# Attention and mixture-of-experts layer on one core: the product with V in two halves of the queries, maxima two tasks further ahead, and two changes merged with it

## The reference

```python
def reference(x, W_qkv, b_qkv, W_out, b_out, w_gate, w1_e, w3_e, w2_e, w1_s, w3_s, w2_s):
    xn = (x - mean(x)) / sqrt(var(x) + 1e-5)
    # attention: 16 heads of 16 channels, 1024 tokens a batch, fp32
    q, k, v = split(xn @ W_qkv + b_qkv)
    q = q * cos + rotate_half(q) * sin; k = k * cos + rotate_half(k) * sin
    attn = softmax(q @ k.T / sqrt(16))
    out = (attn @ v) @ W_out + b_out
    # experts: 16 routed, 4 chosen out of 2 of 4 groups, 2 shared; F = 128
    scores = sigmoid(xn @ w_gate.T)
    w, idx = grouped_top_k(scores)             # 4 a token, weights normalised
    routed = sum over idx of w * (silu(xn @ w1_e.T) * (xn @ w3_e.T)) @ w2_e.T
    shared = (silu(xn @ w1_s.T) * (xn @ w3_s.T)) @ w2_s.T
    return x + out + routed + shared
```

## Time and profile before

| | us |
|---|---|
| median of three runs | 1397.03 (1396.93 to 1402.91) |
| the profiled execution | 1410.99 |
| its span | 1408.4 |
| TensorE busy | 1261.6 (90%) |
| VectorE busy | 1050.5 (75%) |
| ScalarE busy | 735.1 (52%) |
| POOL busy | 506.2 (36%) |

### The profile page before, as it was taken

One profiled execution on the slowest core, in us unless ns is written; L12 is line 12 of the kernel. 1 busy time (PEld: TensorE's weight loads), 2 busy tenths in 40 slices (PEclk: granted clock), 3 DMA queues, 4 the chain that ended last, 5 costly groups with the idle time before them and its releaser, 6 DMA issues. The chain is left out here.

```text
span 1408.4 us, 27771 instructions
## 1 busy us (share of the span) xinstructions
PE 1261.6 (90%) x6717; PEld 645.4 (46%) x6718; DVE 1050.5 (75%) x1715; ACT 735.1 (52%) x1584; POOL 506.2 (36%) x797
## 2 busy tenths in 40 slices
PE   4988927989999999999999999999599999979998
PEld 1544413323333333333333333333488888756665
DVE  5788858868888888888888888888255555537777
ACT  2443311757777777777777777777233333322221
POOL 4665514456132222223131313132277777640000
PEclk9999965989999999999999999999799999989999
DMA  5344453345233213331333223321455555447773
GB/s 176 115 144 147 161 149 84 140 125 177 59 96 78 72 50 95 83 79 48 88 88 76 58 74 95 77 70 53 135 158 157 160 157 159 144 141 233 243 238 127
DMA packets 126755, 169.25 MB, mean 120 GB/s; under 512 B 50109, under 2 KB 98653, under 8 KB 124702
## 3 DMA queue, kind: packets, MB, share of 16 engines
q1 hardware_dynamic: 111358, 126.79, 31.6%
q0 software_dynamic: 15360, 42.04, 9.2%
HBM read 96.58 MB, written 71.64 MB: 119 GB/s over the span
## 5 line engine op out<-in xcount | busy, mean ns | idle before, releaser
L964 DVE TENSOR_REDUCE mx<-pm 128x1 f32<-128x1024 f32 x532 | 626.9, 1219 | 123.6 <-PE pm L1033 113.7
L939 ACT ACTIVATE pr<-pst 128x512 f32<-128x512 f32 x1024 | 535.6, 603 | 228.0 <-PE pst L1057 217.0
L1057 PE MATMUL pst<-qt,kt 50*128 50x512 f32 x1024 | 399.5, 464 | 6.0 <-issue 4.4
L1033 PE MATMUL pm<-kt,qt 48*128 48x512 f32 x1064 | 362.5, 449 | 27.8 <-DVE mx L964 22.1
L1033 PEld LDWEIGHTS pm<-kt,qt 48*128 48x128 f32 x1064 | 169.1, 192 | 275.9 <-DVE mx L964 228.3
L1067 PE MATMUL po<-pr,vt 128*17 128x512 f32 x2048 | 273.7, 607 | 15.0 <-ACT osb L948 12.1
L1057 PEld LDWEIGHTS pst<-qt,kt 50*128 50x128 f32 x1024 | 173.6, 186 | 89.0 <-ACT pr L939 68.4
L1195 POOL DMA_INDIRECT s_y<-ys_c,slot_c x144 | 140.6, 976 | 79.3 <-issue 66.1
L862 POOL CAST mp<-mx 128x16 fp32r<-128x16 f32 x33 | 6.5, 196 | 447.4 <-DVE mx L964 447.4
L1260 PE MATMUL c_pG<-w13s,xt_c 128*128 x576 | 150.1, 384 | 0.0
L884 POOL DMA_INDIRECT s_xg<-p_rows,p_slot x128 | 125.1, 978 | 56.6 <-issue 30.2
(11 more groups left out here) (197 smaller groups left out, 1276.0 us busy)
## 6 DMA issues: line engine op xcount, KB each, us to landing
xg<-s_xg SPq DMA_DIRECT2D x144, 128.5 KB
yg<-s_y SPq DMA_DIRECT2D x32, 512.0 KB, 4.3
kt<-s_k SPq DMA_DIRECT2D x34, 256.0 KB
qt<-s_q SPq DMA_DIRECT2D x68, 128.0 KB
s_q<-stg SPq DMA_DIRECT2D x32, 256.0 KB
s_k<-stg SPq DMA_DIRECT2D x32, 256.0 KB
vt<-s_v SPq DMA_DIRECT2D x17, 272.0 KB, 11.5
w13s<-w SPq DMA_DIRECT2D x1, 4608.0 KB
```

Of the source, the lines that this page charges most:

```text
L939: nc.scalar.activation(pr[:, (k % 2) * 4 + ORDER[i], :], pst[bank(gg, k, i)][:, :], ACT.Exp, scale=SCALE).then_inc(exp_ok, 1)
L964: nc.vector.tensor_reduce(mx[:, half, col:col + 1], pm[slot][:, :, :].rearrange("p a n -> p (a n)"), AX.X, ALU.max).then_inc(mx_free, 1)
L1033: mm = pe.matmul(pm[slot][:, kk, :], qt[buf][rows, half, pair, qi * P:(qi + 1) * P], kt[buf][rows, pair, kk * 512:(kk + 1) * 512], start=T ...
L1057: pe.matmul(pst[bank(buf, k, i)][:, :], kt[buf][rows, pair, kc * P:(kc + 1) * P], qt[buf][rows, half, pair, :], start=True, stop=True)\
```

## The change

Three things are changed together.

1. Stage B. PV runs in two halves of the queries (256 columns each), the first behind the second pair of the quad, the second behind the fourth. The fourth score is issued in its own quad, so each pair holds one half maximum and the score of its own number. The first half waits for all four exponentials of the quad before. The order of the heads is 2, 3, 0, 1. The maxima are 22 tasks ahead, not 20: 23 before the loop, and SWITCH, ROWS1 and ROWS0 come a quad earlier. ScalarE's copy of the output comes behind the fourth exponential of every eighth quad.
2. Stage A. `normalise` moves from VectorE to ScalarE (an activation with bias and scale; VectorE computes the bias in one more operation for the tiles together). The sum of the rotation moves from VectorE to POOL, behind its products.
3. Hand-overs. The tiles that the next stage needs first are placed so that they outlive the stage. SP issues the first eight loads of gathered rows at the end of B ahead of the last store; the wait for the landing of the output stores moves to the start of C on SP; the wait for the last scatters of C moves from POOL to SP in D, ahead of the loads that read them. POOL sends its first tiles in threes, so its last tile is sent earlier in B.

```diff
-AHEAD = 20
+AHEAD = 22
 SWITCH = (32 - AHEAD) // 2
-ORDER = [2, 0, 1, 3]
+ORDER = [2, 3, 0, 1]
...
-            def pv(buf, k, q, u):
+            def pv(buf, k, q, u, part):
-                pe.wait_ge(exp_ok, 4 * (q + 1))
-                if k % 8 == 0:
+                cols = slice(part * QH // 2, (part + 1) * QH // 2)
+                if part == 0:
+                    pe.wait_ge(exp_ok, 4 * (q + 1))
+                if k % 8 == 0 and part == 0:
                     need(pe, osb_ok, u)
                 for h in range(HG):
-                    mm = pe.matmul(po[32 * h:32 * h + VW, :], vt[buf][:, k % 8, h * VW:(h + 1) * VW],
-                                   pr[:, (k % 2) * 4 + h, :], start=(k % 8 == 0), stop=(k % 8 == 7),
+                    mm = pe.matmul(po[32 * h:32 * h + VW, cols], vt[buf][:, k % 8, h * VW:(h + 1) * VW],
+                                   pr[:, (k % 2) * 4 + h, cols], start=(k % 8 == 0 and part == 0), stop=(k % 8 == 7 and part == 1),
                                    tile_position=(0, 32 * h))
...
                                 max_half(mbuf, us[m], slots[m], place(g, k, m), kk)
-                                if m + kk:
-                                    if k % 8 == 0 and m + kk == 1:
-                                        pe.wait_ge(mrow_in[k // 8], 32 * (g + 1))
-                                    scores(gg, k, 2 * m + kk - 1, q)
-                                elif not (isinstance(q, int) and q == 0):
-                                    scores(gg if k else 1 - gg, (k - 1) % QUADS, 3, q - 1)
+                                if k % 8 == 0 and m + kk == 0:
+                                    pe.wait_ge(mrow_in[k // 8], 32 * (g + 1))
+                                scores(gg, k, 2 * m + kk, q)
+                            if k == 1 and m == 0:
+                                pe.wait_ge(v_in[gg], 16 * (j + 1))
+                            if not (isinstance(q, int) and q == 0):
+                                pb, pk = (gg, k - 1) if k else (1 - gg, QUADS - 1)
+                                pv(pb, pk, q - 1, 2 * g + pk // 8 if k else 2 * g - 1, m)
...
                 nc.gpsimd.tensor_tensor(rc[:, sl, :].rearrange("p (h d) -> p h d", d=D), src,
                                         ropesb[:, t, 0:1, :].to_broadcast([P, 2 * H, D]), ALU.mult).then_inc(rc_ok, 1)
+                pool.wait_ge(rs_ok, k + 1)
+                pool.wait_ge(rc_ok, k + 1)
+                need(pool, qrT_ok, k - 1)
+                nc.gpsimd.tensor_tensor(qr[:, sl, :], rc[:, sl, :], rs[:, sl, :], ALU.add).then_inc(qr_ok, 1)
...
-            steps(dve, B, TPB, NT, [(0, normalise), (0, other_stats), (BACK, rest), (ROT, rotate), (TPB, routing)])
+            steps(dve, B, TPB, NT, [(0, other_stats), (BACK, rest), (TPB, routing)])
...
-            steps(act, B, TPB, NT, [(0, root), (BACK, part1), (TURN, turn), (PROJ, take)])
+            steps(act, B, TPB, NT, [(0, root), (0, normalise), (BACK, part1), (TURN, turn), (PROJ, take)])
...
             for i in range(2):
                 sp.wait_ge(plan_out[i], 64 * NT // 2)
+            for k in range(FIRST_XG):
+                load_slots(sp, s_xg, keep, k, k)
             store(FIRST + NG * PER, 1, NG // 2 - 1, 1)
-            for i in range(2):
-                sp.wait_ge(o_out[i], 16 * NG)
...
         def _(sp):
+            for i in range(2):
+                sp.wait_ge(o_out[i], 16 * NG)
             for k in range(EARLY):
                 load_token_tile(sp, x, s_xn, s_o, keep, k, k)
...
-            for i in range(4):
-                wait_alone(pool, y_out[i], 16 * NX // 4, passed)
...
+                if isinstance(k, int) and k == 0:
+                    for i in range(4):
+                        sp.wait_ge(keep["y_out"][i], 16 * NX // 4)
```

More of the change, by code:

```diff
@@ L145, in stage_a @@
         nwt = sb("nwt", [P, NT])
+        shift = sb("shift", [P, NT])
         xt = sb("xt_a", [P, 2, CC, P])
@@ L297, in inverse_root @@
                 own.link(v.tensor_tensor(r_, r_, w_, ALU.mult))
+                own.link(v.scalar_tensor_tensor(out=shift[:, t0:t1], in0=mv[:, t0:t1, 0], scalar=-1.0, in1=r_,
+                                                op0=ALU.mult, op1=ALU.mult))
+                dve.sem_inc(root_ok, 1)
             dve.wait_ge(x_in[0], 16)
@@ L380, in root, with normalise @@
                     nc.scalar.activation(std[:, TPB:NT], var[:, TPB:NT], ACT.Sqrt).then_inc(std_ok, 1)
+            def normalise(k, t, b):
+                if t == 0:
+                    act.wait_ge(root_ok, 1 if isinstance(k, int) and k == 0 else 2)
+                need(act, xT_ok, k - 3)
+                need(act, xn_out[t % 4], (b * TPB // 4 + t // 4) * 16)
+                pick = lambda a: a.rearrange("p a b -> p (a b)")
+                nc.scalar.activation(xn[:, t % 4, :], pick(xs[:, bass.ds(k, 1), :]), ACT.Identity,
+                                     bias=shift[:, bass.ds(k, 1)], scale=rstd[:, bass.ds(k, 1)]).then_inc(xn_ok, 1)
             def turn(k, t, b):
@@ L453, in _ @@
             steps(pe, B, TPB, NT, [(BACK, back), (TURN, turn), (PROJ, project)])
-ROOT_LINKS, ROUTE_LINKS = 5, 42
+ROOT_LINKS, ROUTE_LINKS = 6, 42
 STORES = 4 * PARTS
@@ L723, in stage_b @@
         rec = sb("rec", [P, 16])
-        on = sb("on", [P, 2, 4, HG, D])
+        on, o_out = keep["on"], keep["o_out"]
         ident = keep["ident"]
@@ L739, in stage_b @@
         osb_ok, rec_ok = sem("osb_ok"), sem("rec_ok")
-        o_out = [sem(f"o_out{i}") for i in range(2)]
         pool_own, passed = sem("pool_own_b"), sem("passed_b")
@@ L907, in body @@
                         i = gg * 2 + 1 - half
[L908 to L912, removed]
-                        split(2 * g + 2 - half, half, place(g, SWITCH - 1 if half else SWITCH + 7, 1))
[L914 to L925, removed]
+                        tiles = [(4 * j + 2 + i, i % 2, 2 * j + 1 + i // 2)]
+                        if isinstance(j, int) and j == 0:
+                            tiles = [(n, n % 2, n // 2) for n in range(3 * i - 6, 3 * i - 3) if i > 1]
+                        elif isinstance(j, int) and i > 1:
+                            tiles = []
+                        for tile in tiles[:2]:
+                            fetch(*tile)
+                        split(2 * g + 2 - half, half, place(g, SWITCH - 1 if half else SWITCH + 7, 1))
+                        if isinstance(j, int) and j == 0 and i < 2:
+                            if i == 0:
+                                wait_alone(pool, keep_ok, 2, passed)
+                                plan_places(nc, planned, plan, keep)
+                            else:
+                                send_pads()
+                        for tile in tiles[:2]:
+                            send(*tile)
+                        for tile in tiles[2:]:
+                            fetch(*tile)
+                            send(*tile)
+            body(0)
+            with pool.Fori(1, NG // 2 - 1) as j:
+                body(j)
+            body(NG // 2 - 1)
             for i in range(2):
@@ L940, in body @@
                                                  scale=SCALE).then_inc(exp_ok, 1)
-                            if k % 8 == 1 and i == 0:
+                            if k % 8 == 0 and i == 3:
                                 u = 2 * g + k // 8 - 1
@@ L1124, in _ @@
             rounds(pe, NG // 2, body)
-            scores(1, QUADS - 1, 3, NG * QUADS - 1)
-            pv(1, QUADS - 1, NG * QUADS - 1, 2 * NG - 1)
+            for part in range(2):
+                pv(1, QUADS - 1, NG * QUADS - 1, 2 * NG - 1, part)
             end = FIRST + NG * PER
@@ L1131, with load_slots @@
 BUF_D, EARLY = 8, 4
+FIRST_XG = 8
+def load_slots(eng, s_xg, keep, k, t):
+    eng.dma_start(keep["xg"][:, t, :], s_xg[bass.ds(k * P, P), :]).then_inc(keep["g_in"][t], 16)
 def load_token_tile(eng, x, s_xn, s_o, keep, k, buf):
@@ L1149, in stage_c @@
         w13, w2, eid = keep["w13"], keep["w2"], keep["eid"]
-        slot = sb("slot_c", [P, PER], U32)
-        xg = sb("xg", [P, PER, RW])
+        slot, xg, ys = keep["slot"], keep["xg"], keep["ys"]
         xt = sb("xt_c", [P, 2, CC, P])
@@ L1160, in stage_c @@
         slot_ok = sem("c_slot_ok")
-        g_in = [sem(f"g_in{i}") for i in range(PER)]
-        y_out = [sem(f"yc_out{i}") for i in range(4)]
+        g_in, y_out, o_out = keep["g_in"], keep["y_out"], keep["o_out"]
         xT_ok, xt_ok, gu_ok, sg_ok, hb_ok, hT_ok, ht_ok, yy_ok, ys_ok = (
@@ L1175, in load @@
             def load(k, t, j):
+                if isinstance(k, int) and k < FIRST_XG:
+                    return
                 need(sp, xT_ok, k - PER + 1)
                 need(sp, slot_ok, k - PER + 1)
-                sp.dma_start(xg[:, t, :], s_xg[bass.ds(k * P, P), :]).then_inc(g_in[t], 16)
+                load_slots(sp, s_xg, keep, k, t)
             steps(sp, NX // PER, PER, NX, [(0, load)])
```

33 lines of the change are left out of this document (9 added, 24 removed).

## The result

The changed kernel takes 1444.45 us (median of 4 runs, 1441.51 to 1450.91) where the kernel before takes 1399.07: 1.032 times, 95% interval 1.028 to 1.037. It is 45 us slower; 1339 was forecast. Its profiled execution has a span of 1439.1.

A forecast was written before the change was run, and what follows sets the result against it. No engine was taken as saturated: attention runs round a cycle of waits between TensorE, VectorE and ScalarE. Attention -33, stage A -14, hand-overs -9 and -2 make -58 from 1397: 1339 us, range 1321 to 1380.

The forecast's parts named there:

- The plain quad: Attention quads without a third task: 2.42 us for 2.60, a PV part 0.555, TensorE the bound; a group 43.0.
- Third-task quads: Attention quads with a third task still wait for the second maximum: 3.25 us, as before.
- Rival (b): Attention: a PV part costs 0.63 or more, or VectorE binds at 2.5 and more; 1362 to 1372; chance 0.17.
- Rival (a): Attention: TensorE's issue of a quad's 24 matmuls for 16, each with its load, becomes the bound; about 1490; chance 0.06.
- The loads of the operands at quad 5: Attention: operand buffers switch one quad earlier, so loads are waited for 0.45 us a group, +7 in all.
- Rival (d): Attention: operand loads land late at quad 5, 1.5 us a group and not 0.45; +17, 1356; chance 0.09.
- The first groups: Attention's start: POOL issues third tiles earlier, covered by its 436.6 us of waiting for maxima, so no cost.
- Stage A: Stage A: VectorE gives up the normalising pass and rotation's sum; 4.5 us a tile for the 24 tiles; -14.
- rival (c): Stage A: POOL binds or starves VectorE by their shared port pair; pace stays at 5.0; 1353 or 1356; chance 0.15.
- lower bound: Stage A's best case: tiles at 4.24 us everywhere, -22 in place of -14.
- Hand-overs: Between stages B and C, store to TensorE's start 12.45 to 3.5 us, -9; between C and D, -2.

The follow-up runs named there:

- after_again: The changed kernel, unaltered, run again in the third set beside the kernel before: 1445.5 us, ratio 1.031.
- split24_again: after_split24 run again in the third set, unaltered: 1365.1 us, ratio 0.974 to the kernel before.
- after_split24: The changed kernel with PV in halves only in the 12 quads of each group without a third task, whole in the other 4: 1366.7 us, ratio 0.975.
- before_again: The kernel before, unchanged, run again in the third set for its profile: 1401.1 us, with before at 1402.4.
- s24_best: after_split24 with the rotation's sum back on VectorE and POOL's third merge of maxima ahead of the second eight scatters of vacant slots: 1350.8 us, ratio 0.964.
- whole_best: The changed kernel with PV whole in every quad and the same two repairs as s24_best: 1370.8 us, ratio 0.977.
- before_turn4: The kernel before with TensorE's attention loop rolled as four groups a turn and three turns, for two and seven: 1411.3 us for 1402.7, ratio 1.0075.

## Why the prediction was wrong, point by point

**The plain quad: right.** 2.44 for 2.42, a part 0.56 for 0.555, a group 43.0 for 43.0 in the kernels with 12 quads halved, whose loop body fits. Third-task quads: 3.27, for 3.25; halved too, 3.36. Rival (b) didn't come.

**The step that failed: what the halves cost in instructions.** Rival (a) did see that a quad's instructions go from 32 to 48, but priced the wrong thing, their rate of issue. That rate never bound. What decided is how many the loop holds. At 1766 the loop is fetched anew in each turn, TensorE waits some 8 us at each of six jumps, and two to three quads behind it run at the low clock (the first in 4.27 for 2.66): 3 to 5 more. Quad by quad, after_again has 73 us more than split24_again at its six jumps, 12 each, and 5 more in the quads with a third task (3.36 for 3.27 each); the two kernels differ by 80. Rows for it stood in the profile of before: its page has the row of q8 shown above, with 15 transfers, and their times would have shown that they end when the loop has been gone through once.

The Trainium skill has sizes for this: "Advanced Engine Details and Errata", section "ISA Cache", gives TensorE 128 KB and lines of 16 KB or 256 instructions. The size of the transfers agrees (0.85 MB in 52). An estimate from these figures of the Trainium skill, 128 / 16 x 256, lets 2048 instructions fit, and 1766 would have; here 1702 didn't and 1638 did, about a line and a half less, so the measurement decides. Nor do the changed kernel's 8.8 transfers a turn agree with its body, which by the Trainium skill's 256 instructions a line is 6.9 lines long; what the other two bring isn't shown. The forecast didn't weigh any of it.

**The loads of the operands at quad 5: oversized.** +7 was taken; in split24's groups quad 4 or 5 takes at most 0.4 longer, and only in some. Rival (d) didn't come.

**The first groups: a term at nothing that isn't.** That POOL's 436.6 us of waiting for maxima cover its earlier tiles was read from a sum over the whole loop. In the second group POOL is busy with the vacant slots, and its merge for quad 5 comes late. TensorE's wait in after_split24:

```profile
306.33 1.05 PE L1078 MATMUL po<-pr,vt 128*17 128x512 f32 x8
317.80 0.61 PE L1048 MATMUL pm<-ident,mp 128*32 128x128 f32 x2 [10.42 <-POOL mp L865]
318.33 0.79 PE L1040 MATMUL pm<-kt,qt 48*128 48x512 f32 x1
```

The kernel before has it too in another execution (8.83 in before_again), so it is less a cost of the change than a floor under its gain: what TensorE gains ahead of that point it would give back there. That is argued from these two waits; s24_best, in which POOL's work was moved, took 3 us less over the first three groups.

**Stage A: -14 forecast, 0 measured; rival (c).** POOL's sum itself was as priced (1.308 for 1.31) and the tiles run at 4.22 wherever they run, but in each batch one takes 11.4 to 11.9 us, which is about as much above 4.22 as the slow tiles of a batch of before are together (8.8, 4.8 and 6.1). The waits of the changed kernel from 26 to 181:

```profile
DVE stg L346 <- ACT stg L412: 39.5, 11, 7.1
POOL rs L259 <- ACT qks L393: 34.8, 11, 15.7
...
PE pR L451 <- DVE stg L346: 14.6, 3, 5.0
```

And the timeline at one such place, VectorE's two subtractions, drawn-out operations between them and TensorE behind:

```profile
70.36 0.69 DVE L346 TENSOR_TENSOR stg<-pR,stg 128x512 fp32r<-128x512 f32 x1
...
71.70 1.24 DVE L471 TENSOR_TENSOR g_bq<-g_ms,g_top 128x128 f32<-128x128 f32 x1
...
77.07 1.36 DVE L543 TENSOR_TENSOR g_ms<-g_c 128x128 f32<-128x128 f32 x1
...
81.47 0.68 DVE L346 TENSOR_TENSOR stg<-pR,stg 128x512 fp32r<-128x512 f32 x1
...
82.21 1.11 PE L451 MATMUL pR<-ident,qr 128*128 128x128 f32 x4 [4.77 <-DVE stg L346]
```

VectorE's subtraction for the stores starts at 70.36 and next at 81.47: eleven us of routing operations, up to 1.36 each, stand ahead of it, and TensorE waits. In the window from 59.7 to 180 the same 151 instructions of routing hold VectorE for 80.4 us where they took 66.6, and for 70.3 (160 instructions) in s24_best, which has the sum on VectorE. This is the mechanism of (c), which had a chance of 0.15. Giving the sum back to VectorE won 5 us of the 14. What holds the rest isn't shown by a run; another wait in each batch, of ScalarE for the store of v (4.1 to 4.7 us, 2.9 to 5.1 before), is in both kernels. (The lower bound that the prediction gave for this stage, -22, comes to -20.5 by its own rows; nothing hangs on it.)

**Hand-overs: right.** 10.8 for 9, and 1.5 for 2.

**The sum.** From 1339: +80 (the jumps, and the halves of the third-task quads), +14 (stage A), -7 (operand loads), -1 (hand-overs) and +2 (before at 1399 for 1397) make 1427; 17 us are left. The durations of the groups in the profiles of before_again and split24_again show 14 of them. The first three groups took 151.9 us together and take 156.0, where the forecast had them 7 shorter: 11. The other thirteen gain 2.55 each, for 2.75: 3. The second group alone takes 65.6 for 59.5. It differs between executions, 54.0 in the profile of before, from which the forecast was made, 60.3 in that of the changed kernel and 62.5 in that of after_split24, so part of the 11 may be chance.

**What stays open.** The standstill: it came in two of five sets of runs, once on a chip that had been free of it minutes before. With it the kernels with 12 quads halved take 1479 to 1489 us for 1365 to 1367, and before takes 1417 for 1402. Its cause was not found; that it follows denser work on TensorE fits, but is only argued. In such a set of runs whole_best, not s24_best, would be the kernel to have; that was not run.

## What to carry to other kernels

Count the instructions of a loop body before splitting work inside it: the same split that gains 0.16 us a quad lost 80 us when TensorE's loop body grew from 1638 to 1766, and leaving four useless splits a group out turned +3% into -2.5%. Look at the times of the instruction transfers: they must end after the first turn. An engine's idle time over a whole loop doesn't cover a wait in one group, and an operation moved off a busy engine can slow what remains there.

## What the runs showed of the hardware

At a jump back to a loop that is fetched anew TensorE stood for 3.1 us (before_turn4) or for 2.5 and 5.1 (the changed kernel), and two to three quads behind it ran at the low clock (4.27 us for 2.66). TensorE's loop of 1702 instructions was fetched anew each turn, the one of 1638 was not. Operations of VectorE of 128x128 took up to 1.36 us beside a busy POOL, where others of their shape took 0.28 to 0.29. And TensorE can stand still for some 3 us, with matmuls begun and none ending, followed by 2 to 4 quads at the low clock, in some sets of runs and not in others.
